# Grouped attention of a macaron block: the order of its small steps, and the engine that forms the negative maximum

## What is computed

```
b, sq, _ = x.shape
q = jnp.einsum('bsh,he->bse', x, w_q).reshape(b, sq, GROUPS, HPG, KVC)     # 16 heads of 128, 4 groups
kv = jnp.einsum('bsh,he->bse', x, w_kv)
k, v = jnp.split(kv, 2, axis=-1)
scores = jnp.einsum('bqgpd,bkgd->bgqpk', q, k) * SCALE
scores = jnp.where(causal[None, None, :, None, :], scores, -jnp.inf)
probs = jax.nn.softmax(scores, axis=-1).astype(x.dtype)
ctx = jnp.einsum('bgqpk,bkgd->bqgpd', probs, v).reshape(b, sq, HEADS * KVC)
return jnp.einsum('bse,eh->bsh', ctx, w_dense)
```

## Time and profile before

| | |
|---|---|
| median of 3 runs | 998.9 us (996.7 to 1003.71) |
| the profiled execution: its own time | 998.63 us |
| its span, first to last instruction | 996.6 us |
| mean granted TensorE clock | 0.991 of full |
| grouped attention, first scores to last PV | about 597 to 926 us |
| PE busy over the whole span | 90% |

### The profile page before, as it was taken

How to read it: one execution, slowest core, us unless ns; L and a number is a source line. 1 busy time by engine, 2 the same in 40 slices (tenths; PEclk the granted TensorE clock), 3 DMA queues, 4 the chain that set the end, 5 groups by cost and what they waited for, 6 DMA issues and landing times. The chain is left out here.

```text
span 996.6 us, 19557 instructions
## 1 busy us (share of the span) xinstructions
PE 899.9 (90%) x7309; PEld 601.5 (60%) x7334; DVE 744.6 (75%) x1803; ACT 577.8 (58%) x1102; POOL 173.7 (17%) x131
## 2 busy tenths in 40 slices
PE   3999989999999999999998988899999989998897
PEld 2787743334433433468876765676666766766686
DVE  7846877888888888245468666888888888888654
ACT  5534223566666766744446546767676666766263
POOL 4010130052344145000014500000000000000154
PEclk9999999999999999999999999999999999999999
DMA  5020343453255330203101003667776676766101
GB/s 117 1 88 0 110 122 61 77 104 70 57 107 92 66 77 24 66 1 112 58 1 43 0 1 64 128 120 119 118 122 119 107 132 114 122 123 122 25 1 43
DMA packets 176918, 75.60 MB, mean 76 GB/s; under 512 B 154648, under 2 KB 172744, under 8 KB 175304
## 3 DMA queue, kind: packets, MB, share of 16 engines
q1 hardware_dynamic: 176824, 74.36, 36.7%
HBM read 30.53 MB, written 5.85 MB: 37 GB/s over the span
## 5 line engine op out<-in xcount | busy, mean ns | idle before, releaser
L1010 ACT ACTIVATE PT<-bank 128x512 f32<-128x512 f32 (+2 forms) x320 | 154.4, 559 | 101.9 <-PE bank L1419 83.8
L1908 DVE CUSTOM_DVE_ANT_0 bank<-bank,stripS 128x128 f32<-128x128 f32 (+1 forms) x224 | 129.8, 604 | 28.1 <-PE bank L1343 27.0
L1614 PE MATMUL pair<-KH,QH 128*128 128x512 f16 (+3 forms) x576 | 115.3, 328 | 30.4 <-DVE QH L2019 17.4
L1087 ACT ACTIVATE P<-pair,nm 128x1024 f32<-128x1024 f32 (+7 forms) x128 | 94.5, 738 | 80.9 <-DVE nm L2051 80.7
L1658 PE MATMUL bank<-PT,VH 128*128 128x128 f16 x1728 | 117.7, 219 | 2.9 <-DMA PT<-PS 2.9
L1658 PEld LDWEIGHTS bank<-PT,VH 128*128 128x128 f16 x1728 | 99.4, 98 | 22.5 <-issue 15.7
L1343 PE MATMUL bank<-KT,QT 96*128 96x512 bf16 (+2 forms) x336 | 103.0, 331 | 10.3 <-DVE MX L1908 8.4
L767 POOL TENSOR_TENSOR rstd<-veps,mhalf 128x4 f32<-128x4 f32 x12 | 12.2, 1020 | 557.3 <-DVE veps L1765 557.3
L2077 DVE SCALAR_TENSOR_TENSOR PS<-P,rec,PS 128x1024 f16<-128x1024 f32 (+7 forms) x128 | 102.8, 804 | 5.9 <-ACT PS L1109 4.1
L1822 DVE TENSOR_TENSOR hf<-sil,bank 128x512 f32<-128x512 f32 x64 | 43.9, 686 | 83.6 <-PE bank L1167 52.4
L2047 DVE TENSOR_REDUCE mx<-pair 128x1 f32<-128x1024 f32 (+7 forms) x128 | 96.0, 750 | 7.8 <-PE pair L1616 7.7
(11 more groups left out here) (185 smaller groups left out, 1753.8 us busy)
## 6 DMA issues: line engine op xcount, KB each, us to landing
KT<-qk_dram SPq DMA_DIRECT2D x21, 192.0 KB
stripS<-band_rows SPq DMA_DIRECT2D x28, 128.0 KB, 2.1
qk_dram<-parts SPq DMA_DIRECT2D x12, 256.0 KB, 2.2
stripT<-seq_dram SPq DMA_DIRECT2D x27, 88.0 KB, 8.4
q_raw<-w_gu SPq DMA_DIRECT2D x4, 512.0 KB, 10.1
w_raw<-w_dense SPq DMA_DIRECT2D x2, 1024.0 KB, 6.9
w_raw<-w_q SPq DMA_DIRECT2D x2, 1024.0 KB, 4.8
PT<-PS SPq DMA_TRANSPOSE x128, 3.6
```

Source lines behind the costliest of these rows:

```text
L1010: act.activation(PT[:, n % 4, hs[0]:hs[-1] + 1, 0:ni], src, ACT.Exp).then_inc(s["s2_exp"], 1)
L1087: act.activation(exps(n), pair[n % 2][:, 0:P * (ib + 1)], ACT.Exp, bias=nm1[:, n % 2:n % 2 + 1], scale=SCALE1, accum_out=den1[:, n % 2:n % ...
L1614: ins = pe.matmul(out, QH1[:, h % 2, l, P * ib:P * (ib + 1)], KH1[:, r, h // (H1 // GR), HALF * c:HALF * c + nj], start=(i == 0), stop=(i ...
L1908: dve.tensor_tensor_reduce(out, out, stripS[:, h, HALF - nj:HALF], 1.0, LOWEST, ALU.add, ALU.max, mx).then_inc(s["s1_max"], 1)
```

## The change

1. `nm1` moves from DVE to ACT: an activation Copy with an immediate scale, 128x1, in front of the exp and waited for by it.
2. On ACT, the order in an iteration becomes: `nm1`, exp, key/value piece, context piece, high half, query piece. (The context piece was ahead of the exp.)
3. Query pieces on PE go to places 0 and 2. ACT evicts them in the next iteration, DVE two iterations after ACT (places 3 and 5).
4. The low part of a context piece goes to DVE two iterations after ACT's high part (places 3 and 7), except for the last two pieces.
5. Dense pieces go to places 4 and 6 of an even head, and both remaining ones to place 4 of an odd head.
6. The last four key/value pieces are formed one at a time in iterations 0 to 3, in place of two each in iterations -1 and 0.

```
-        Q_AT = (1, 5)
+        Q_AT = (0, 2)
         HI_LAG, LO_LAG, PV_LAG, CT_LAG = 1, 2, 5, 6
-        DENSE_FROM = TB + TB // 2 + CT_LAG + 1
-        DENSE_AT = (0, 4, 8, 9)
+        DENSE_FROM = TB + TB // 2 + CT_LAG + 2
+        DENSE_AT = {0: (0,), 2: (1,), 8: (2, 3)}
...
-            return [(k // (2 * TB), DENSE_AT.index(k % (2 * TB)))] if 0 <= k and k % (2 * TB) in DENSE_AT else []
+            return [(k // (2 * TB), c) for c in DENSE_AT.get(k % (2 * TB), ())] if k >= 0 else []
+
+        def ct_low_at(n):
+            return [q for q in range(STEPS // 4) if n == 4 * q + 3 + CT_LAG + (2 if q < STEPS // 4 - 2 else 0)]
...
# ScalarE
                 def scores(n):
                     ib = block_of(n)
+                    act.wait_ge(s["sc_mx"], n + 1)
+                    if n >= 2:
+                        act.wait_ge(s["sc_exp"], n - 1)
+                    act.activation(nm1[:, n % 2:n % 2 + 1], mx1[:, n % 2:n % 2 + 1], ACT.Copy, scale=-SCALE1).then_inc(s["sc_nm"], 1)
                     act.wait_ge(s["sc_nm"], n + 1)
...
                 for n in range(-1, LAST):
+                    if 0 <= n < STEPS:
+                        scores(n)
+                    if 1 <= n < 5:
+                        keys_high(KV_AHEAD + n - 1)
                     if 0 <= n - CT_LAG < STEPS and (n - CT_LAG) % 4 == 3:
...
-                    if n in (0, 1):
-                        keys_high(KV_AHEAD + 2 * n)
-                    if 0 <= n < STEPS:
-                        scores(n)
-                    if n in (0, 1):
-                        keys_high(KV_AHEAD + 2 * n + 1)
...
# TensorE
-                    if n < 1:
-                        for t in range(KV_AHEAD + 2 * (n + 1), KV_AHEAD + 2 * (n + 2)):
-                            keys_values(t)
+                    if 0 <= n < 4:
+                        keys_values(KV_AHEAD + n)
...
# VectorE
-                    dve.wait_ge(s["sc_mx"], n + 1)
-                    if n >= 2:
-                        dve.wait_ge(s["sc_exp"], n - 1)
-                    dve.tensor_scalar(nm1[:, n % 2:n % 2 + 1], mx1[:, n % 2:n % 2 + 1], -SCALE1, None, ALU.mult).then_inc(s["sc_nm"], 1)
...
-                    if n in (0, 1):
-                        for t in range(KV_AHEAD + 2 * n, KV_AHEAD + 2 * n + 2):
-                            keys_low(t)
+                    if 1 <= n < 5:
+                        keys_low(KV_AHEAD + n - 1)
...
-                    if n >= 1:
-                        for h, c in q_at(n - 1):
+                    if n >= 3:
+                        for h, c in q_at(n - 3):
                             queries_low(h, c)
-                    if 0 <= n - CT_LAG < STEPS and (n - CT_LAG) % 4 == 3:
-                        q = (n - CT_LAG) // 4
+                    for q in ct_low_at(n):
```

## The result

The changed kernel takes 973.46 us (median of 4 runs, 972.66 to 974.85) against 999.26 us before (996.7 to 1003.71): a ratio of 0.9739, 95% interval 0.9702 to 0.9775, so 22 to 30 us less. The forecast was 978, in a range of 971 to 990.

The account below looks back on a forecast made before the run. PE's 23.0 us of waits in the grouped attention were what could be gained: 998.63 less 23.0, plus 0.6 for odd heads, 0 at both ends, gives 976.2; 976.5 against the median, 1.5 for handovers, forecast 978, range 971 to 990.

Parts of the forecast that it names:

- What bounds: Grouped attention: PE's idle time is 15.9 us waiting for queries' low parts and 7.1 us for exps, together 23.0 us.
- Query pieces at places 0 and 2: Removes PE's 14 query waits (15.9 us) and DVE's 22.3 us of waits for ACT; first piece fills the 1.01 us hole.
- `nm` on ACT: DVE loses 0.15 us a step; ACT's operation takes 0.28 us to exp's start; chain from maximum to exp grows 0.22 to 0.32.
- Following one head: Timing one steady head: 18.2 us against 20.07, slack 0.15 us at 7-block and 0.14 at 6-block scores, PE setting the time.
- Context low parts and dense pieces: Context low parts two iterations later cost nothing, with up to 0.5 us exposed each second head if DVE falls behind.
- Transposes: Transposing DMA lands 2.3 to 6.0 us after issue; the median is covered, the slowest landings are not.
- rival 1: Tight ACT chain keeps part of the waits: `nm` at 0.50 us, plus slow DMA landings; 983 to 990 us, chance 0.25.
- First two heads: Key/value pieces one by one: head 1 starts about 1 us later, gives back as much; taken at 0, from -3 to +3.
- Number 4: Rival: the chain maximum, `nm`, exp, scores paces every step, 0.1 us more in each of 128; 1012 us, chance 0.05.
- Number 3: Rival of no effect: DVE bounds after all, its waits only moved; 993 to 1003 us, chance 0.05.
- rival 2: More gained: ACT's price at 0.2 us and first two heads better by 3; 973 to 975 us, or 971; chance 0.10.
- main case: New order removes PE's waits and PE sets the time; forecast 978, 974 to 982 us, chance 0.55.

Follow-up runs that it names:

- a1: Changed kernel with the negative maximum (`nm`) put back on DVE, all other edits kept: 974.25 us, 0.9744 of the kernel before.
- a2: Kernel before with only the negative maximum (`nm`) moved to ACT: 1000.57 us, 1.0013 of the kernel before.
- a4: Changed kernel with the query pieces' low part on DVE in the same iteration as ACT's high part: 1018.87 us, 1.0186 of the kernel before.
- a3: Kernel before with only the query pieces moved to places 0 and 2, low part on DVE two iterations after ACT: 982.28 us, 0.9834.
- b1: Changed kernel with one additional 128x1 copy on ACT before `nm` in each step, waited for: 982.61 us, 0.9856 of the kernel before.
- b2: Changed kernel with three additional 128x1 copies on ACT before `nm` in each step: 1027.11 us, 1.0293 of the kernel before.
- c3: Changed kernel with dense pieces at old places and context low parts in the iteration of their high parts: 990.81 us, 0.9918 of the kernel before.
- b4: Changed kernel with dense pieces at old places (3 and 7 of even heads, 3 and 4 of odd): 981.51 us, 0.9839 of the kernel before.
- b3: Changed kernel with the context's low part on DVE in the same iteration as ACT's high part: 989.24 us, 0.9908 of the kernel before.
- c2: Changed kernel with the last four key/value pieces as before, two each in iterations -1 and 0: 974.18 us, 0.9759 of the kernel before.
- c4: Changed kernel with the last head's dense pieces at places 0 and 2 and the first head's key/value low parts after the low half: 969.41 us, 0.9724.
- c1: Changed kernel with the context piece ahead of `nm` and exp on ACT, as before: 979.21 us, 0.9808 of the kernel before.

## Why the prediction was right, step by step

- **What bounds.** That PE's 23.0 us of waits were nearly all there was to gain in the steady part, and that both kinds would go, was right: heads 2 to 14 lost 22.3 us, where 22.1 lie in them and 21.5 are left after the 0.6 given back (the other 0.9 of the 23.0 is the wait at the end of head 1). a1 and a2 show that they went by the order.
- **Query pieces at places 0 and 2.** Right for the gain, but calling what the low parts' distance frees "DVE time freed which PE doesn't see at once" undersold it: a4 shows that without it the change is 45 us worse. a3 shows that the query pieces with their distance are worth 15 us from the first scores on (399.6 to 384.6), not all of it.
- **`nm` on ACT.** Taken at 0.28 us from start to start between bounds of 0.16 and 0.5; it is 0.203 us long and 0.24 from start to start. That it is free and slightly risky was right (b1, b2). The rule of the Trainium skill ("ScalarE: Activation LUTs", Rules for kernel authors), to do multiplies on VectorE, does not decide here: a1, where the operation stays on VectorE, takes the same time.
- **Following one head.** The head came out at 18.2 in the steady part (18.1 and 18.2 in turn). The slack of the 6-block scores is 0.13 us for 0.14. That of the 7-block scores, 0.15, came out at nothing in even heads and 0.23 in odd ones: the following had left out that the context's low part stands before the 8-block maximum in every second head. The wait of 0.09 at the end of odd heads shrank to about 0.02: the next scores start 0.06 us, the handover, after the exp is read, and 0.20 us after PE's last PV starts, where it is 0.18 at the end of even heads. Both places have no slack left; that no visible wait came of it is luck.
- **Context low parts and dense pieces, "costed at nothing".** Right as a cost of the change, within the 0.24 us by which the low part at place 7 delays the 8-block maximum, but they are not neutral: taking them back costs 13.3 and 7.0 us. They had to move for the query pieces' gain to arrive in full. The following of the head had them at their new places, so the sum was right without my knowing what they were for.
- **Transposes.** The slow landings (2.4 to 6.3 us now) let ACT wait 3.1 us in 6 places and PE 1.0, and made three heads longer, 0.15 us a head on average. The sum had nothing for them; rival 1 had up to 0.4.
- **First two heads.** The sum has 0.9 us of gain here, the wait at the end of head 1, and 0 beside it; measured are 1.6 us, so the term of 0 should have been 0.7. Head 1 does start later by its own clock (23.95 us after head 0, against 23.43), about half of the 1 us that I had; but head 1 gives back 2.1 us (16.51 against 18.65), with that 0.9 in it.
- **The distance of 4.5 us between 978 and 973.5.** The added 1.5 us for handovers didn't come. 0.95 us were gained ahead of the stage, which the change doesn't touch: that is luck. 0.7 are the first two heads, 0.8 lie in heads 2 to 14, mostly the 0.6 given back for odd heads, and 0.55 from head 15 on, taken at nothing.
- **Rivals.** Number 4 (each step's chain is the pace) is refuted by b1: 9 us for 0.24 us a step, not 31. Number 3 (DVE bounds) by a1, where DVE keeps all its work and PE is still at 99%. Number 1's mechanism exists and starts at once beyond the present cost (b1); `nm` was cheaper than it needed. By its number, 973.5, the result lies in rival 2's 973 to 975 and just under the 974 to 982 of the main case. Of rival 2's two reasons the first came true for `nm` (0.24 us from start to start, 0.2 supposed) but isn't what gained, as a1 takes the same time without it, and the second at 1.6 us of its 3. The mechanism is that of the main case, with most of its small terms put too high or left out.

## What to carry to other kernels

Where an engine near full waits at fixed points of a regular loop, write down for each wait whether it is a hole (nothing to do beside a long chain) or a late piece, and move side pieces from the second to the first; what an engine's total work is says little, as a1 and a2 show, as long as it stays clear of the length of the round (b2 is where ACT's doesn't). When a value goes through two engines in order, let the second take it some iterations after the first (here two; one was not tried): in the same iteration it makes its whole queue wait for the other's (45 us for the queries, 13 for the contexts). Test such edits in pairs, since one can be worth nothing, or a loss, without the other.

## What the runs showed of the hardware that was not expected

The granted clock has dips in stages whose instructions are the same in all these kernels, and they differ from one profiled execution to the next. In the stretch from 130 to 150, of the kernel before, the changed kernel, and c3:

```profile
130.00:150.00 20.00, 18.52 (x151) 9.45 (x151) 14.09 (x22) 4.53 (x7) 9.92 (x9) 0.91 0.44 117
```

```profile
130.00:150.00 20.00, 18.45 (x163) 9.19 (x164) 15.53 (x23) 4.64 (x7) 9.92 (x9) 1.00 0.49 124
```

```profile
130.00:150.00 20.00, 18.30 (x112) 8.77 (x110) 11.90 (x19) 4.74 (x7) 9.92 (x9) 0.66 0.34 96
```

PE is busy for as long but gets through 151, 163 and 112 matmuls. The first scores start at 597.0, 596.1 and 600.9 us; in the other kernels they start at 595.3 to 595.9 with 1.00 (a1, a3, b1, b4), 596.8 to 597.6 with 0.91 (b2, b3, c2, c4), 599.3 and 599.4 with 0.83 (a4, c1), 600.4 with 0.66 (a2). It is not a property of the kernel: two executions of a1 (order only) took 971.73 and 972.15 us at a mean granted clock of 0.993 over the run, the two others 976.36 and 976.66 at 0.986. So up to 5 us of a difference between two executions can lie in stages that no edit touched; c1's profiled execution carries 3.3 us of it against the changed kernel's, and c3's 4.9. What makes the clock dip in one execution and not in the other stays open.

A 128x1 activation, for which the trace of before had no row, takes 186 to 210 ns; the line of the changed kernel:

```profile
L1088 ACT ACTIVATE nm<-mx x128: 186/203/210, 598.9 to 892.3; 128x1 f32<-128x1 f32 x128
```
